# A state-space, FP8 and mixture-of-experts stack on one core: a PSUM bank for the serial stage, two instead of three for gate and up, and softplus sums on GpSimd

## The reference

```python
# layer 0: selective scan (Mamba), 256 inner channels, 16 states
xi, res = split(x @ in_proj_w.T)
xi = silu(causal_depthwise_conv(xi, 4 taps))
dt, Bm, Cm = split(xi @ x_proj_w.T)               # 64, 16, 16
delta = softplus(dt @ dt_proj_w.T + dt_proj_b)
h = exp(delta * A) * h + delta * Bm * xi          # scan over time, per channel and state
y = (sum over states of h * Cm + xi * D) * silu(res) @ out_proj_w.T
# layer 0 ffn: both operands rounded to FP8 (e4m3), x @ w.T + bias
# layer 1: delta = mean over features of softplus(x @ W_delta.T + b_delta)
#          a scan of 16 states over time, y = h @ C.T + D * x
# layer 1 ffn (MoE): router softmax over 8 experts, top 2, capacity 512 per expert
#          expert: gelu(h @ Wg) * (h @ Wu) @ Wd + x, hidden size 256; h is the RMS norm of x
#          tokens beyond capacity take a small side net (hidden size 64) instead
```

## Time and profile before

| | us |
|---|---|
| median of three runs | 481.6 |
| the profiled execution, its own time | 480.05 |
| its span, first to last instruction | 478.3 |
| VectorE (DVE) busy | 408.9, 85% |
| TensorE (PE) busy | 407.7, 85% |
| ScalarE (ACT) busy | 319.4, 67% |
| GpSimd (POOL) busy | 230.5, 48% |
| DMA moved | 74.2 MB |

### The profile page before, as it was taken

The page is one execution under the profiler, slowest core; times in us unless marked ns, Lnnn a source line. Parts: engine busy times, 40 slices in busy tenths (PEclk is TensorE's granted clock), DMA queues, the critical chain, the costliest instruction groups (busy, mean ns, idle before and its releaser), DMA issues.

```text
span 478.3 us, 6017 instructions
## 1 busy us (share of the span) xinstructions
PE 407.7 (85%) x1680; PEld 246.4 (52%) x1680; DVE 408.9 (85%) x890; ACT 319.4 (67%) x521; POOL 230.5 (48%) x203
## 2 busy tenths in 40 slices
PE   4989777679268999999967799999496999999993
PEld 3333222243124777755423478766132687778873
DVE  4569999999999999999999889999989765675654
ACT  3887246458544999999963778874746579587231
POOL 0049599899574475456964724656962000000000
PEclk9989989999597999999997599999789899999997
DMA  8496398998245455556853723575750000000000
GB/s 288 168 332 223 110 302 292 320 311 277 86 176 187 166 175 177 181 161 194 275 185 105 248 88 120 165 229 158 251 200 2 0 1 0 3 0 23 1 1 22
DMA packets 22065, 74.19 MB, mean 155 GB/s; under 512 B 2320, under 2 KB 4368, under 8 KB 21648
## 3 DMA queue, kind: packets, MB, share of 16 engines
q1 hardware_dynamic: 22032, 73.82, 46.7%
HBM read 72.50 MB, written 1.31 MB: 154 GB/s over the span
## 4 chain that ended last, share of the span: by engine, by line
PE 50%; DVE 26%; issue 11%; ACT 7%; POOL 4%; DMA 2%; SPq 1%; DVEq 0%; ACTq 0%; POOLq 0%
PE ps_g L719 11%; PE ps_y L626 10%; PE ps_u L764 10%; DVE ps_state L1127 7%; PE ps_u L719 6%; DVE product L1144 4%; PE ps_state L719 2%; DMA hidden<-w_up 2%; DVE drive L1127 2%; POOL drive L999 2%; DVE delta L1111 2%; DVE delta L1113 2%; PE ps_y L764 1%; POOL product L1020 1%; DVE stats L1154 1%
## 5 line engine op out<-in xcount | busy, mean ns | idle before, releaser
L999 POOL TENSOR_TENSOR drive<-du,b_row 128x512 f32<-128x512 f32 x128 | 164.9, 1308 | 51.0 <-DVE ps_state L1127 37.3
L626 PE MATMUL ps_y<-product,par 128*128 128x512 f32 x256 | 135.6, 648 | 21.1 <-DVE product L1144 12.7
L865 ACT ACTIVATE ps_state<-delta,decay_rate 128x512 f32<-128x512 f32 x128 | 85.5, 688 | 58.3 <-DVE product L1144 45.2
L626 PEld LDWEIGHTS ps_y<-product,par 128*128 128x128 f32 x256 | 47.9, 204 | 81.8 <-issue 32.7
L782 ACT ACT_TABLE_LOAD x69 | 88.5, 1283 | 1.9 <-PEq L1385 0.7
L1020 POOL TENSOR_TENSOR product<-drive,c_row 128x512 f32<-128x512 f32 x38 | 48.4, 1274 | 55.3 <-DVE drive L1127 51.3
L1144 DVE TENSOR_TENSOR product<-ps_state,c_row 128x512 f32<-128x512 f32 x90 | 60.2, 679 | 1.3 <-PE ps_y L626 1.0
L764 PEld LDWEIGHTS ps_u<-wd,hidden 128*128 128x128 f32 x448 | 53.8, 192 | 4.9 <-issue 2.0
L1127 DVE TENSOR_TENSOR_SCAN ps_state<-ps_state,carry,drive 128x512 f32<-128x512 f32 x44 | 55.3, 1274 | 0.3 <-ACT ps_state L865 0.3
L1127 DVE TENSOR_TENSOR_SCAN ps_state<-ps_state,drive 128x512 f32<-128x512 f32 x46 | 54.6, 1213 | 0.9 <-ACT ps_state L865 0.8
L764 PE MATMUL ps_u<-wd,hidden 128*128 128x128 f32 x448 | 54.9, 276 | 0.0
(11 more groups left out here) (253 smaller groups left out, 600.5 us busy)
## 6 DMA issues: line engine op xcount, KB each, us to landing
b_row<-bc_dram SPq DMA_DIRECT2D x64, 512.0 KB, 5.0
c_row<-bc_dram SPq DMA_DIRECT2D x64, 512.0 KB, 4.1
x_in<-x_t SPq DMA_DIRECT2D x4, 256.0 KB, 6.9
gelu<-w_gate SPq DMA_DIRECT2D x1, 1024.0 KB, 9.1
hidden<-w_up SPq DMA_DIRECT2D x1, 1024.0 KB, 10.9
wd<-w_down SPq DMA_DIRECT2D x1, 1024.0 KB, 12.8
out<-acc SPq DMA_DIRECT2D x4, 256.0 KB, 2.4
par<-params SPq DMA_DIRECT2D x1, 598.0 KB, 6.6
```

Of the source, the lines that this page charges most:

```text
L626: mm(ps_y[:, :], ident, product[:, g % PRODUCTS, :], start=False, stop=(n == STATE - 1)).then_inc(y_pe, 1)
L865: nc.scalar.activation(ps_state[g % RING][:, :], delta[:, c % 2, h, :], ACT.Exp, scale=decay_rate[:, h, n:n + 1]).then_inc(decay_act, 1)
L999: nc.gpsimd.tensor_tensor(drive[:, g % DRIVES, :], du[:, h, :], b_row[:, m % ROWS, n % 2, :], ALU.mult).then_inc(drive_pool, 1)
```

## The change

- **Banks.** The eight banks are now `ps_y`, three `ps_state`, `ps_tail`, two `ps_net`, `ps_acc`. Every tail step writes and reads `ps_tail`. Gate and up groups rotate through two banks (five in the last chunk). Tail step 0 waits only until the counts of the tail before are read.
- **The tail's steps.** With one bank, the steps that held several banks at once follow one another: the input of the small scan is copied out by ScalarE (`bx`), `dlt`, `bx` and `mean` come one after another, and x3 is read out before the RMS norm, which is then made by a multiplication of x3 (`hn`). Tail has one step more (16). The softplus temporaries move from `gelu` and `hidden` to tiles of the tail.
- **Softplus sums.** 1 + e is made by ScalarE (`one`), the remainder by one VectorE operation. The two sums with relu and logarithm go to GpSimd (`settle` for delta in chunks 1 to 3, tail step 7 in chunks 0 to 2); in chunk 0 and in the last tail they stay on VectorE.
- **Products.** `MULTIPLIED` has 8, 8, 10 and 16 units on GpSimd for chunks 0 to 3, where it had 8, 10, 10 and 10. The product ring is 7 instead of 8, the gelu ring 2 instead of 3.
- **Order.** All five lists of `PLACES` are new (not shown). On VectorE, the statistics of chunk 1's tail (`tail 1`, step 1) now stand after step 3 of chunk 2 (before: after step 12), and the last `accum` of chunk 0's MoE after step 15 of chunk 2 (before: step 7).

```diff
-PRODUCTS = 8
+PRODUCTS = 7
-MULTIPLIED = (QUARTER, THIRD, THIRD, THIRD)
+MULTIPLIED = (QUARTER, QUARTER, THIRD, ODD)
-GROUP = 3
+GROUP = 2
...
-        ps_g = [bank("ps_g0"), bank("ps_g1")]
-        ps_u = [bank("ps_u0"), bank("ps_u1")]
-        ps_acc = ps_u[1]
+        ps_tail = bank("ps_tail")
+        ps_net = [bank("ps_net0"), bank("ps_net1")]
+        ps_acc = bank("ps_acc")
-            return (*ps_g, *ps_u, *ps_state)[k] if c == 0 else (ps_u[0], ps_g[0])[k % 2]
+            return (*ps_net, ps_tail, ps_acc, *ps_state)[k] if c == 0 else ps_net[k % 2]
-            return [*net_banks, *ps_state] if c == LAST else net_banks
+            return [*ps_net, *ps_state] if c == LAST else ps_net
...
# TensorE, tail
-                    if c == LAST:
-                        pe.wait_ge(product_dve, count(by_vector, STEPS - 1))
-                        pe.wait_ge(state_dve, STEPS)
-                    elif c:
-                        pe.wait_ge(hidden_dve, 2 * NETS * c)
-                        pe.wait_ge(gelu_act, 2 * NETS * c)
-                        pe.wait_ge(acc_dve, NETS * c)
+                    if c:
+                        after(pe, tail_dve, c - 1, "late")
...
+                if k == 8:
+                    after(pe, tail_act, c, "bx")
+                    l1_made(pe, c)
+                    mm(ps_tail[0:STATE, :], mean_w[:, :], l1_sp[:, :], start=True, stop=True).then_inc(tail_pe.sem, 1)
+                if k == 9:
+                    after(pe, tail_act, c, "decay")
+                    after(pe, tail_dve, c, "drive")
...
# ScalarE, pre
+                    if c >= 2:
+                        act.wait_ge(decay_act, UNITS * (c - 1))
+                        act.wait_ge(du_pool, HALVES * (c - 1))
+                    do(pre_act, delta[:, q, h, :], sp_exp[:, :], ACT.Identity, bias=1.0)
                     do(pre_act, sp_ln[:, h, :], sp_exp[:, :], ACT.Ln, bias=1.0)
...
# ScalarE, tail
+                if k == 8:
+                    after(act, tail_pe, c, "bx")
+                    copy(tail_act, l1_drive[:, :], ps_tail[0:STATE, :])
...
+                if k == 11:
+                    after(act, tail_dve, c, "sh3")
+                    normalise(tail_act, x3, lambda j: block_of(ps_tail[:, :], j), rstd, shift)
...
+                if k == 12:
+                    after(act, tail_act, c, "rms")
+                    for j in range(BLOCKS):
+                        last = nc.scalar.mul(hn[:, j, :], x3[:, j, :], rms[:, j:j + 1])
...
# GpSimd
+            def settle(c, h):
+                q = c % 2
+                if c == 0:
+                    return
+                after(pool, rest_dve, c, f"rest{h}")
+                after(pool, pre_act, c, f"relu{h}")
+                nc.gpsimd.tensor_tensor(delta[:, q, h, :], sp_relu[:, h, :], delta[:, q, h, :],
+                                        ALU.subtract).then_inc(delta_pool.sem, 1)
+                after(pool, delta_pool, c - 1, f"b{h}")
+                after(pool, pre_act, c, f"ln{h}")
+                nc.gpsimd.tensor_tensor(delta[:, q, h, :], delta[:, q, h, :], sp_ln[:, h, :],
+                                        ALU.add).then_inc(delta_pool.sem, 1)
...
+                if k == 7 and c < LAST:
+                    after(pool, tail_dve, c, "rest")
+                    after(pool, tail_act, c, "relu")
+                    nc.gpsimd.tensor_tensor(l1_sp[:, :], l1_relu, l1_sp[:, :], ALU.subtract).then_inc(l1_pool.sem, 1)
+                    after(pool, l1_pool, c, "b")
+                    after(pool, tail_act, c, "ln")
+                    nc.gpsimd.tensor_tensor(l1_sp[:, :], l1_sp[:, :], l1_ln, ALU.add).then_inc(l1_pool.sem, 1)
...
# VectorE, make_delta
-                do(pre_dve, v.tensor_scalar(delta[:, q, h, :], sp_exp[:, :], 1.0, -1.0, ALU.add, ALU.add))
-                own(pre_dve, c, f"t{h}")
-                do(pre_dve, v.tensor_tensor(delta[:, q, h, :], sp_exp[:, :], delta[:, q, h, :], ALU.subtract))
-                own(pre_dve, c, f"a{h}")
-                do(pre_dve, v.tensor_tensor(delta[:, q, h, :], delta[:, q, h, :], sp_relu[:, h, :], ALU.add))
-                own(pre_dve, c, f"b{h}")
+                after(dve, pre_act, c, f"one{h}")
+                do(rest_dve, v.scalar_tensor_tensor(delta[:, q, h, :], delta[:, q, h, :], 1.0, sp_exp[:, :],
+                                                    ALU.subtract, ALU.subtract))
+                if c:
+                    return
```

More of the change, by code:

```diff
@@ L280, in build @@
         product = sb("product", [P, PRODUCTS, CHUNK])
-        def l1_of(c, name):
-            name = {"ln": "abs", "t": "sp"}.get(name, name)
-            i = L1_NAMES.split().index(name)
-            if c == CHUNKS - 1:
-                place = product[:, i, :]
-            elif i < 6:
-                place = gelu[:, i // 2, i % 2, :]
-            else:
-                place = hidden[:, 1, 0, :]
-            return place[0:STATE, :] if name in ("step", "decay", "drive") else place
         carry = sb("carry", [P, HALVES, STATE])
@@ L414, in build @@
         tail_pe = Marks(sem("tail_pe"), "r1 x1t ffn x2t dlt bx mean r3 hnt logits counts")
-        tail_act = Marks(sem("tail_act"), "l1 rstd1 x1 x1q ffn l2 rstd2 x2 x2t abs exp relu ln step decay "
-                         "l3 rstd3 l4 rms hn hnt hi x3 exps acc")
-        tail_dve = Marks(sem("tail_dve"), "st1 mo1 sh1 r2 st2 mo2 sh2 t a b sp drive scan keep st3 mo3 vr msq sh3 inv s3 "
-                         "f3 lo lg top cen tot tinv probs sort where wf p1 p2 picked late over kept w0 w wsum xw red psum pbef")
+        tail_act = Marks(sem("tail_act"), "l1 rstd1 x1 x1q ffn l2 rstd2 x2 x2t abs relu exp one ln bx decay "
+                         "l3 rstd3 x3 l4 rms hn hnt hi exps acc")
+        tail_dve = Marks(sem("tail_dve"), "st1 mo1 sh1 r2 st2 mo2 sh2 rest drive scan keep st3 mo3 sh3 vr msq inv "
+                         "lo lg top cen tot tinv probs sort where wf p1 p2 picked late over kept w0 w wsum xw red psum pbef")
         tail_pool = Marks(sem("tail_pool"), "bias")
+        l1_pool = Marks(sem("l1_pool"), "b sp")
+        l1_dve = Marks(sem("l1_dve"), "b sp")
         gate_pe = sem("gate_pe")
@@ L430, in after, with delta_made, l1_made @@
             eng.wait_ge(marks.sem, marks.done(c, name))
+        def delta_made(eng, c, h):
+            if c == 0:
+                after(eng, first_dve, 0, f"delta{h}")
+            else:
+                after(eng, delta_pool, c - 1, f"delta{h}")
+        def l1_made(eng, c):
+            if c == LAST:
+                after(eng, l1_dve, 0, "sp")
+            else:
+                after(eng, l1_pool, c, "sp")
         def tokens(c):
@@ L693, in tail @@
                     after(pe, tail_dve, c, "picked")
-                    after(pe, tail_act, c, "x3")
                     for j in range(BLOCKS):
-                        o = tail_bank(c, "counts")[:, j * EXPERTS:(j + 1) * EXPERTS]
+                        o = ps_tail[:, j * EXPERTS:(j + 1) * EXPERTS]
                         mm(o, before[:, :], picked[:, j, :], start=True, stop=False)
@@ L755, in down @@
                 if e == 0:
-                    after(pe, tail_dve, c, "late")
-                    if c == LAST:
+                    if c:
                         pe.wait_ge(acc_dve, NETS * c)
@@ L827, in pre @@
                     if c and h == 0:
-                        after(act, pre_dve, c - 1, "delta1")
+                        delta_made(act, c - 1, 1)
                     do(pre_act, sp_abs[:, h, :], pre_bank(c, k)[:, :], ACT.Abs, bias=dt_b[:, h:h + 1])
@@ L835, in pre @@
                     if h:
-                        after(act, pre_dve, c, "a0")
+                        after(act, rest_dve, c, "rest0")
                         after(act, pre_act, c, "ln0")
@@ L853, in step @@
                 if n == 0:
-                    after(act, pre_dve, c, f"delta{h}")
+                    delta_made(act, c, h)
                 if g == 0:
@@ L926, in tail @@
                     rsqrt(tail_act, c, var_log[:, :], "l4", mean_sq[:, :], eps[:, 1:2], rms[:, :])
-                if k == 11:
-                    after(act, tail_dve, c, "f3")
-                    normalise(tail_act, hn, lambda j: block_of(tail_bank(c, "r3")[:, :], j), scale3, shift3)
                 if k == 12:
+                    after(act, tail_act, c, "rms")
+                    for j in range(BLOCKS):
+                        last = nc.scalar.mul(hn[:, j, :], x3[:, j, :], rms[:, j:j + 1])
+                    last.then_inc(tail_act.sem, 1)
+                if k == 13:
                     after(act, tail_pe, c, "hnt")
@@ L1033, in pair @@
                                         product[:, g % PRODUCTS, :], ALU.add).then_inc(pair_pool, 1)
-            run("gpsimd", du=make_du, step=step, multiply=multiply, pair=pair, tail=tail)
+            run("gpsimd", settle=settle, du=make_du, step=step, multiply=multiply, pair=pair, tail=tail)
         @block.vector
```

151 lines of the change are left out of this document (71 added, 80 removed), and 198 rows, old and new, of the table PLACES.

## The result

The changed kernel takes 461.2 us (median of 4 runs, 459.3 to 462.0) against 481.5 us of the kernel before in the same comparison; the ratio is 0.958, with a 95% interval of 0.953 to 0.962. The forecast was 467.5, the range 453 to 483: the direction and the range hold, the gain is 20 us where 13 to 14 were forecast.

The account below looks back on a forecast made before the run. VectorE was taken to bound the kernel up to 374 us, TensorE after. The terms, 480.05 - 1.5 - 15 + 0.6 + 3 = 467.2, led to a forecast put at 467.5 us, range 453 to 483 with rivals.

Parts of the forecast that it names:

- The bound: Up to 374 us VectorE is busy nearly throughout, so time saved on it counts there and not after.
- The work removed: VectorE before 374 us: 16.3 from delta softplus, 6.7 from tail sums, 2.7 from products, 25.7 us in all.
- First stretch: 30 to 105 us: of 4.0 us removed from VectorE, 1.5 us gained (0 to 4), GpSimd and DMA being near full.
- From there to the last scan: 105 to 374 us: 21.7 us of VectorE work removed, a gain of 15 us (8 to 22).
- VectorE's idle time grows from 11.8 to 18.5 us: 105 to 374 us: allowance for longer waits with VectorE and TensorE so full and each queue in order.
- near 94%: 105 to 374 us: TensorE, busy 233.2 of 269 us, would be 94% busy if the stretch shrank to 249 us.
- +0.6 us for the start: Chunk 0, before the scans: each half's logarithm comes one operation later, uncovered, costing 0.6 us.
- What order and bank are worth: 105 to 374 us: the tail's own bank and new order let the removed VectorE work shorten TensorE's full stretches (101 us).
- Two banks after the scans: Third MoE, after 374 us: two uncovered gaps from ScalarE's detours with two gate/up banks, +3 us (0 to 9).
- 1 (all lands, 455): Before 374 us: all removed VectorE work becomes gain, idle time staying as it is; 455 us, chance 0.20.
- 2 (two banks starve TensorE, 488): MoEs of chunks 0 to 2: TensorE waits at ScalarE's detours, 1.6 us each; 488 us, slower, chance 0.15.
- 3 (GpSimd's sums come late, 478): Deltas and tails: nine pairs of GpSimd sums stand on the path, returning 22.9 us; 478 us, chance 0.15.

Follow-up runs that it names:

- sums_back: The changed kernel with all 18 softplus sums (12 delta, 6 tail) moved from GpSimd back to VectorE; 476.0 us, ratio 0.994.
- delta_back: The changed kernel with only the 12 delta sums of chunks 1 to 3 back on VectorE, tail sums left on GpSimd; 473.1 us, ratio 0.982.
- before_less_vector: The kernel before with one VectorE operation replacing each softplus's four in chunks 1 to 3 and tails 0 to 2, values differing; 463.3 us, ratio 0.965.
- before_sums_pool: The kernel before, old banks, orders and product split, with only the softplus sums on GpSimd and ScalarE adding the one; 485.0 us, ratio 1.016.
- fewer_products: The changed kernel with 4 of chunk 3's 16 GpSimd products moved back to VectorE; 464.3 us, ratio 0.970.
- before_reordered: The kernel before with its three gate and up banks, only TensorE's gate and up order changed to two gate, two up; 479.9 us, ratio 0.998.

## Why the prediction was right, and where its sizes were off

**The bound.** That VectorE bounds the time up to the last scan is borne out twice: by sums_back and delta_back, and in the kernel before by before_less_vector (17.9 us for 23.7). That its work can be handed to GpSimd at little cost is true of the changed kernel and false of the old order (before_sums_pool).

**The work removed.** 25.7 us were forecast; VectorE's busy time fell from 408.9 to 385.0, 23.9 us, of which 20.6 lie between the first and the last scan, 1.8 ahead of the first and 1.5 behind the last. The remainder operation was taken at 1.17 us and has 1.129. Its 128x512 operations from float32 to float32, scans left out, fell by more, from 153.4 to 125.7 us in sum over the whole span; other groups grew a little, the 28 tensor_tensor of 128x32 from 6.4 to 7.6 us for one.

**Where it lands: two terms mis-sized, which cancel in part.** First stretch: -1.5 forecast, -3.6 measured (chunk 0's scans, 62.4 to 58.8), that is nearly all of the 4.0 held possible. From there to the last scan: -15 forecast, -17.4 measured. The forecast was 21.7 us of work removed less 6.7 us of idle time added. Measured between the first scan of chunk 1 and the last scan, VectorE's busy time fell by 15.6 us (262.44 to 246.80) and its idle time by 1.8 (11.7 to 9.9). So the work removed was taken 6 us too high: the softplus operations gave 16.8 us there (17.5 forecast) and the products 2.0 (4.1 forecast), and the rest of VectorE's busy time grew by some 3. The failed step is the one in which VectorE's idle time grows from 11.8 to 18.5 us "with two engines this full": it shrank. That the two errors, 6 and 8.5 us, point opposite ways is luck, and makes the forecast look better than its terms. TensorE was not near 94% either: it is busy 227.51 of these 256.7 us, 89%, for in the kernel before part of its busy time was a low clock (0.92 there, 0.96 after). The term of +0.6 us for the start can't be read: the first scan starts at 34.6 to 38.2 us in the traces of these kernels, two of them executions with an unchanged start, 35.56 and 38.14.

**What order and bank are worth.** The prediction called them what lets the removed work show. Themselves they bring little: before to sums_back is +2.7, +4.8, -3.8 and -7.2 us in the four chunks, and of the last, six products fewer on VectorE would explain most (four of them cost 4.0 us in fewer_products). But in the old order two banks cost 26 us, with 11.8 us of waits for readers where the new one has 1.4, and GpSimd's sums 24 us in place of 4 to 5. Which part of the change permits this is open: the tail's own bank, the order, the split of the products and the places of the sums were not tried one by one.

**Two banks after the scans.** +3 forecast; +0.9 measured from the last scan to the end against the trace of the kernel before (106.2). That trace is the slowest of four with the old order and three banks: the others have 103.1 (before_sums_pool), 104.5 (before_reordered) and 104.5 (before_less_vector), while nearly all traces with the new order have 107.1 or 107.2. So the end grew by 1 to 4 us, and a size of 3 is not refuted; its cause is, since TensorE's gate and up groups wait 2.0 us there, and a third bank takes nothing off. From the third MoE's first gate group (350.62) to the end it is 108.5 us, not 107, and the new order leaves four identity products behind that group instead of one; the last scan is the better mark.

**Rivals.** 1 (all lands, 455): the time lies midway between it and the forecast. Its condition, idle time as it was, came true; its price did not, since 20.6 and not 25.7 us of busy time left the scans. 2 (two banks starve TensorE, 488): its 24 us are near the 26 measured in the old order, but by chance: they were priced as ScalarE's detours, and of the 11.8 us of waits seen 8.1 are for VectorE. In the new order the waits are nearly absent; whether for the reason given against it was not tried. 3 (GpSimd's sums come late, 478): its 22.9 us are near the 24 measured in the old order, but VectorE waited 1.3 us for drives there and 14.7 in the tails; in the new order no such waits are left and only the contention is, 4 of its "17 at most".

**The other checks.** VectorE 385.0 (383 forecast), GpSimd 258.0 (258), table loads 65. The clock stays at 0.94 or more between the MoEs but for 0.89 from 96 to 154 us: the forecast's 0.9 is just missed. The first two MoEs have TensorE full in one stretch only (46.00 of 46). Two slips of the prediction change nothing: TensorE's idle time between 105 and 374 us is 35.8 us by its own rows, not the 32 given for rival 1, and 467.2 with the median's 1.5 on top would be 468.7, not 467.5.

## What to carry to other kernels

When an engine that is full hands work to another whose queue is in order, price the work at the receiver twice: by how near full it is in that stretch (here GpSimd took a first load of sums at a fifth of its length and a second one, at the same places, at three quarters), and by what stands behind it in its queue. The same sums cost 24 us in the old order and 4 in the new, with its banks, places and split of products, so an order should be judged by what it makes cheap, not by what it saves alone. And a sum for such a change is better made by stretch than by idle time held in reserve.

## What the runs showed of the hardware

A VectorE operation with two SBUF inputs does not merely wait for the GpSimd instruction that runs when it starts. It took 5.44 us (0.69 alone) in sums_back, as long as four back-to-back GpSimd multiplications (4.92), and the remainder in delta_back took 5.42 at the same place. The Trainium skill (SBUF — State Buffer, Who interferes with whom) says that such an instruction contends with a GpSimd one that reads SBUF and that the one that comes first keeps the ports for the whole instruction. The traces agree, with more: in these two cases VectorE did not get its turn between GpSimd's instructions in a row. A third lies between: the remainder at 50.30 us in sums_back took 2.24 us, past the end of the GpSimd multiplication that ran and of the next. It is not always so: the remainder at 122.30 us in sums_back came in between two GpSimd multiplications (1.38 us), and the second of them then took 1.72 us instead of 1.26. What decides is open.

Size does not protect: two of eight 128x32 operations of 0.19 us took 1.32 and 1.30 us when GpSimd's products were moved beside them, about the length of one GpSimd instruction (1.26).
